# The last batch's gate and up pieces moved later, and three engines' batch loops written out

## The reference

```python
x = L0_attn_x
xn = _layernorm(x, axis=-1)
x = x + _L0_attn_ref(xn, W_attn, b_attn, W_proj, b_proj) + _L0_ffn_ref(xn, w_gate, w_up, w_down)
```

## Time and profile before

| | |
|---|---|
| median of 3 runs | 3677.69 us (3674.8 to 3678.53) |
| the profiled execution, its time | 3676.18 us |
| its span, first to last instruction | 3674.3 us |
| TensorE matmuls busy | 3603.0 us (98% of the span) |
| VectorE busy | 2613.4 us (71%) |
| ScalarE busy | 1191.0 us (32%) |
| GpSimd busy | 1080.1 us (29%) |
| mean granted TensorE clock | 0.997 |

### The profile page before, as it was taken

One profiled execution on the slowest core, in us unless ns is written; L12 is line 12 of the kernel. 1 busy time (PEld: TensorE's weight loads), 2 busy tenths in 40 slices (PEclk: granted clock), 3 DMA queues, 4 the chain that ended last, 5 costly groups with the idle time before them and its releaser, 6 DMA issues.

```text
span 3674.3 us, 61753 instructions
## 1 busy us (share of the span) xinstructions
PE 3603.0 (98%) x20748; PEld 2603.4 (71%) x20748; DVE 2613.4 (71%) x3834; ACT 1191.0 (32%) x2249; POOL 1080.1 (29%) x542
## 2 busy tenths in 40 slices
PE   8999999999999999999999999999999999999999
PEld 6557557557566565575575588888888888888887
DVE  6775766766766666767667677777777777777776
ACT  2542532533524514415325322222222222222222
POOL 0760851843825816708508500000000000000000
PEclk9999999999999999999999999999999999999999
DMA  6525535336346255255356511001110011101110
GB/s 198 131 76 174 114 103 178 82 122 173 76 139 164 63 186 129 79 185 115 101 170 170 181 40 34 31 29 34 34 34 30 30 34 34 32 28 34 34 34 29
DMA packets 180518, 336.89 MB, mean 92 GB/s; under 512 B 42688, under 2 KB 50368, under 8 KB 179392
## 3 DMA queue, kind: packets, MB, share of 16 engines
q1 hardware_dynamic: 156096, 280.47, 26.9%
q10 hardware_dynamic: 24192, 53.49, 4.3%
HBM read 213.92 MB, written 118.43 MB: 90 GB/s over the span
## 4 chain that ended last, share of the span: by engine, by line
PE 89%; issue 3%; DMA 3%; DVE 2%; POOL 1%; ACT 1%; SPq 1%; ACTq 0%; DVEq 0%; POOLq 0%
PE f_ps L1556 26%; PE ps_dense L1042 13%; PE f_ps_o L1568 13%; PE ps_st L1099 8%; PE ps_s L1067 5%; PE ps_dense L1213 5%; PE ps_y L1125 4%; PE ps_dense L1125 4%; PE ps_dense L1137 2%; DMA arena<-mr 1%; PE f_ps L1548 1%; PE ps_dense L1067 1%; PE ps_st L1108 1%; PE ps_s L1072 1%; PE ps_st L1002 1%
## 5 line engine op out<-in xcount | busy, mean ns | idle before, releaser
L1556 PE MATMUL f_ps<-wgu,xqt 128*128 128x512 f32 (+1 forms) x4608 | 991.7, 373 | 1.4 <-DVE xqt L1416 1.4
L1556 PEld LDWEIGHTS f_ps<-wgu,xqt 128*128 128x128 f32 x4608 | 841.6, 188 | 122.8 <-DVE xqt L1416 1.8
L956 ACT ACTIVATE pt<-ps_st 128x512 f32<-128x512 f32 (+3 forms) x1152 | 537.9, 526 | 502.9 <-PE ps_st L1099 344.6
L672 DVE TENSOR_REDUCE mx<-ps_s 128x1 f32<-128x640 f32 (+3 forms) x512 | 523.8, 1023 | 166.2 <-PE ps_s L1072 164.9
L1568 PE MATMUL f_ps_o<-wd,hqt 128*128 128x512 f32 x2112 | 512.1, 395 | 0.6 <-DVE hqt L1442 0.6
L1568 PEld LDWEIGHTS f_ps_o<-wd,hqt 128*128 128x128 f32 x2112 | 392.0, 188 | 79.5 <-DVE hqt L1442 0.8
L1042 PE MATMUL ps_dense<-arena,wa 128*128 128x512 f32 x1536 | 385.4, 400 | 12.9 <-DVE stage L725 6.9
L604 POOL TENSOR_TENSOR stage<-stage,pt 128x1536 f32<-128x1536 f32 (+2 forms) x128 | 378.8, 2959 | 16.7 <-ACT pt L956 6.4
L602 POOL TENSOR_TENSOR stage<-pt 128x1792 f32<-128x1792 f32 x48 | 192.8, 4016 | 620.0 <-ACT pt L956 564.4
L1042 PEld LDWEIGHTS ps_dense<-arena,wa 128*128 128x128 f32 x1536 | 282.1, 190 | 75.8 <-issue 10.6
L672 DVE TENSOR_REDUCE mx<-ps_dense 128x1 f32<-128x128 f32 (+3 forms) x424 | 204.4, 482 | 104.5 <-PE ps_dense L1072 104.5
(11 more groups left out here) (145 smaller groups left out, 5303.3 us busy)
## 6 DMA issues: line engine op xcount, KB each, us to landing
qk_scratch<-stage SPq DMA_DIRECT2D x128, 512.0 KB, 2.8
stack<-qk_scratch SPq DMA_DIRECT2D x192, 256.0 KB
arena<-qk_scratch SPq DMA_DIRECT2D x192, 256.0 KB
xs<-in_L_attn_x SPq DMA_DIRECT2D x64, 256.0 KB, 3.5
rob<-in_L_attn_x ACTq DMA_DIRECT2D x64, 256.0 KB, 2.8
acc_scratch<-rob ACTq DMA_DIRECT2D x64, 256.0 KB, 2.2
xt<-in_L_attn_x SPq DMA_DIRECT2D x64, 256.0 KB, 2.6
at<-acc_scratch SPq DMA_DIRECT2D x64, 256.0 KB, 2.6
```

The source lines that it names most:

```text
L672: nc.vector.tensor_reduce(mx[:, h * ST + q:h * ST + q + 1], scores_bank(p, n)[:, 0:(q + 1) * P], axis=AX.X, op=ALU.max, negate=True).then_ ...
L956: nc.scalar.activation(exps(kt)[:, heads[0], q - kt * P:q - kt * P + n], ps_st[:, w % ST_RING, 0:n], ACT.Exp, scale=SCALE).then_inc(st_exp, 1)
L1556: last = nc.tensor.matmul(ps[:, SLOT[c], gu, 0:n].rearrange("p (j n) -> p j n", n=P), xqt[:, a, k], wgu[:, b, gu * FC + f // P:gu * FC + ( ...
```

## The change

TensorE's, VectorE's and ScalarE's batches are written out without a loop; SyncE and GpSimd keep theirs. The wait of QK0 and QK1 for the batch before is now for seven and for all eight of its sums, and falls away in the first batch. In the last batch the pieces of gate and up are issued after the first key tile of a pair, none in pairs 0 and 1, one each in pairs 2, 3 and 4, two in pair 5, one in pair 6 and two in pair 7.

```diff
-    PIECE_AT = [2, 1, 1, 1, 1, 0, 0, 0]
+    PIECES_AT = [(), (), (0,), (1,), (2,), (3, 4), (5,), (6, 7)]
...
+    def batches_in_line(body):
+        for b in range(B):
+            body(b, b == B - 1)
+
+    def batches_and_rest_in_line(body):
+        for first, end, matrix, unit in REST:
+            for b in range(first, end):
+                body(b, False, (matrix, unit - first))
+        body(B - 1, True, None)
...
-        batches(dve, body)
+        batches_in_line(body)
...
-                    if final and kt == PIECE_AT[p]:
-                        shared.load_gate_up(act, p)
+                    if final and kt == 0:
+                        for piece in PIECES_AT[p]:
+                            shared.load_gate_up(act, piece)
...
-        batches_and_rest(act, body)
+        batches_and_rest_in_line(body)
...
                 if n < 0:
-                    pe.wait_ge(o_sum, ONE + b * ST)
+
+                    if b:
+                        pe.wait_ge(o_sum, ONE + (b - 1) * ST + ST + n + 1)
                     return
...
-        batches(pe, body)
+        batches_in_line(body)
```

## The result

The changed kernel takes 3646.73 us in the median of four runs (3644.24 to 3647.5), the kernel before, run beside it, 3676.24 us (3674.16 to 3678.53): ratio 0.9917, 95% interval 0.9901 to 0.9933. That is 29.5 us less; a second measurement, on another chip (e11), gives 24.9 us less (0.9928). The forecast of 3656.7 us, 21 us less, is 10 us off, and the time lies 4 us under the low end of the range. The profiled execution took 3647.5 us (span 3645.7, granted clock 0.997), 28.7 us less than that of before.

What follows compares the result with a forecast made beforehand. TensorE is busy nearly everywhere, so only its idle times can be gained: 10.05 + 6.0 + 4.9 = 20.95 us off the profiled 3676.18 us gives 3655.2 us, a median of 3656.7 us; range 3651 to 3664 us.

Steps and rivals of the forecast that it cites:

- ScalarE's jumps: At five of seven batch boundaries, ScalarE's pause at its loop's jump back goes: 10.05 us less, lower bound 6.9 us.
- TensorE's and VectorE's jumps: At the batch boundaries, removing these two engines' own jumps gains nothing; bound 0.08 us per boundary, 0.5 us for six.
- The pieces: In the last batch's pair 1, the maxima transfer no longer stalls beside piece 0: 4.9 us less, bounds 3.3 and 5.3.
- The signs named: If right: boundary stretches some 47.8 us, no projection idle time for L720 or L725, no 4 us ScalarE pause there.
- The burst of pair 7: Last batch, pair 7: 3,072 KB under way make VectorE's reciprocal 1.8 us late, covered by up to 2.86 us, costing nothing.
- Inside the pairs I expect nothing either: Inside the batches' pairs of heads: no gain, since a straight-line pair takes 18.66 us and a looped one 18.61 us.
- Rival (c): Insides of batches gain too, from register instructions that vanish: 0.8 us a batch, 3651 us; chance 0.06.
- QK0's wait: At seven batch boundaries, QK0 waiting for seven sums instead of eight gains 6.0 us; bounds nothing and 8.7 us.

Runs made afterwards that it cites:

- e11: The changed kernel run again unaltered, on another chip: 3648.89 us, ratio 0.9928 to the kernel before.
- e2: The kernel before with only ScalarE's batches written out without a loop: 3666.23 us, ratio 0.9983.
- e3: The kernel before with only the pieces of gate and up moved to their new places: 3667.46 us, ratio 0.9982.
- e9: The kernel before with 128 identity transposes ahead of TensorE's first work, moving its code by a whole packet: 3675.77 us, ratio 1.0003.
- e1: The kernel before with only TensorE's batches written out without a loop, old wait of QK0 kept: 3661.85 us, ratio 0.9965.
- e10: The kernel before with only VectorE's batches written out without a loop: 3675.85 us, ratio 1.0002.
- e6: The changed kernel with the pieces of gate and up back at their old places: 3652.32 us, ratio 0.9939.
- e4: The kernel before with 64 identity transposes ahead of TensorE's first work, moving its code by half a packet: 3674.59 us, ratio 0.9998.
- e7: The changed kernel with 64 identity transposes ahead of TensorE's first work, moving its code by half a packet: 3648.48 us, ratio 0.9930.
- e5: The changed kernel with QK0 waiting again for all eight sums of the last batch: 3656.32 us, ratio 0.9952.
- e12: The changed kernel with the third unit of the last batch one product later on every engine, second measurement: 3641.56 us, ratio 0.9912.

## Why the prediction was wrong

**What held.** ScalarE's jumps: 10.05 us forecast. The mechanism is shown (e2: every boundary at 48.7 us), the size is that of one execution; against e3 and e9 it is 6.5 us, by e2's medians 7.2. TensorE's and VectorE's jumps: nothing forecast, 0.08 us a boundary (e1) and nothing that can be measured (e10). The pieces: 4.9 us forecast, 4.55 alone (e3) and 5.2 taken out of the changed kernel (e6). The 5.3 us of the stage table agree with 4.9 by luck, since 4.1 - 0.9 + 2.0 us are in them. The signs named came true: boundaries of 47.6 us, no idle time of the projection. The burst of pair 7 went as argued; in the timeline of the changed kernel:

```profile
2024.53 0.82 ACTq L1375 DMA_DIRECT2D wgu<-wq_scratch  x2
...
2033.23 3.47 POOL L615 TENSOR_TENSOR stage<-stage,pt 128x1536 f32<-128x1536 f32 x1
2035.00 0.25 DVE L704 RECIPROCAL inv<-den 128x16 f32<-128x16 f32 x1 [5.22 <-DMA den<-rob]
2035.17 1.81 DVE L1422 TENSOR_SCALAR xd<-xt,norm_stats 128x512 f32<-128x512 f32 x1
```

The 1024 KB piece landed in 9.4 us (9.8 estimated) and the denominators in 3.8 instead of 1.7 us. The reciprocal waits 5.22 instead of 3.64 us, 1.6 us more (1.8 estimated), and the instruction behind it takes 1.81 instead of 3.40 us, the same 1.6 us back.

**The step that failed** is "Inside the pairs I expect nothing either". It was priced at zero from one pair, 18.61 us in the looped batch against 18.66 in the last one. That pair has index 2, one of the three (2, 4, 5) where no packet of code meets the maxima. Two of the eight pairs, 3 and 6, did lose 0.4 to 1.1 us in every looped batch, and in sum 269.89 - 261.15 = 8.7 us of the 9.0 come from them. Rival (c) had the sign, with 0.8 us a batch instead of 1.3 and another cause, the registers' instructions that vanish. The cause is shown by e1, e4 and e9: packets of TensorE's program started where they made the maxima late.

It is not that the loop repeats a bad place and written-out code doesn't. Written out, the packets too start at nearly the same place in every batch, only at another one. In us behind the start of the pair:

| packets of q8, batches 0 to 6 | before | after |
|---|---|---|
| pair 1 | 0.6 to 1.0 | 1.6 to 2.3 |
| pair 3 | 2.8 to 3.3 | 12.3 to 12.9 |
| pair 6 | 2.9 to 3.5 | 3.1 to 4.9 |

(The first packet of each pair; pairs 1 and 3 before, and some others, have one more, near the pair's end.) In pair 6 the new place is a near miss: in e11, which is the same program, the packet starts at 2.8 us in batch 1, the transfer lands in 3.3 us and the pair takes 18.97 instead of 18.65 us. In pair 1 a packet now makes the maxima land in 2.4 to 3.3 us, for which TensorE doesn't wait. So the 9 us came with the place that the new code happened to get, not with the loop's absence: e4 has them with every loop in place, e7 gives 3.3 of them back without one. That the place was a good one is luck.

The row was to be seen before: L1099's waits for `arena<-mr` sum to 7.1 us over 17 times, and no step of the forecast spoke of them.

**A size that was off.** QK0's wait was taken at its idle time, 6.0 us; it was worth 7.9 (e5), since TensorE's busy time at the boundaries was longer with it too.

**What stays open.** The feed-forward part behind its first tile takes 2.3 us more in both profiles of the changed kernel, and 1546.5 to 1547.5 us in those of e5, e7 and e12, so the change as such doesn't explain it. The granted clock does for the most part: in the first 24.5 us of that part its mean is 0.88 in the changed kernel and 0.92 before, in the last 20.7 us 0.84 and 0.89 (1.00 in e12). An estimate from these: 0.04 x 24.5 + 0.05 x 20.7 = 2.0 us. Why it falls there was not tried. How a packet of code slows a transfer of 8 KB on another queue (the engines' turns, or memory) is not shown either, nor why one that starts 1.6 to 1.7 us behind the second issue left it at 1.8 to 2.1 us in the changed kernel, while at 1.7 to 1.9 us before it landed in 3.8 to 3.9.

## What to carry to other kernels

A stretch that repeats should be compared in all its repetitions, not in one: group the waits by line first, and give each row of several microseconds a sentence, even when the change isn't aimed at it. Writing a loop out moves where its code is fetched, for better or worse; where small transfers with no slack sit on the path, a hundred-odd instructions without use ahead of the loop tell within one run whether the code's place matters. A wait that is taken away can be worth more than its idle time, here 1.3 times (7.9 for 6.2 us). And a time read from one execution, like the 10.05 us for ScalarE's jumps, should be read from several before a sum rests on its second digit.

## What the runs showed of the hardware

A 16 KB packet of TensorE's program that started 1.2 to 1.9 us behind the issue of an 8 KB transfer went with a landing in 3.2 to 3.9 instead of 1.8 us, in all 14 places of the kernel before; an 8 KB packet of VectorE's program 1.2 to 1.4 us behind it went with 2.8 us (e7, e10). A load of 1,280 KB made the same kind of transfer land in 5.0 to 5.6 us. ScalarE's jump back went with a pause of 4.04 us at the boundary of the earlier trace rows, and cost the kernel 1.3 to 2.0 us each time (6.5 to 10.05 us for five), TensorE's 0.08 us. Half a packet of extra code at the start took 10.55 us out of the looped batches, and the last batch was 8.5 us longer in the same profile (e4).
